# A new order for the first tile and for the end of attention, score blocks two in a row, and a second tile with plain fp32 projections

## The reference, cut to what matters

```python
x = x + tanh(g_xattn) * attention(layernorm(x), ctx, ctx, ctx)
x = x + tanh(g_ffn) * (layernorm(x).reshape(-1, 512) @ w.T)

def attention(q, k, c, s):
    qp = Wq @ instance_norm(q) + bq
    kp = Wk @ instance_norm(k) + bk
    sp = Ws @ s + bs
    attn = softmax(qp.T @ kp, axis=-1)          # 512 x 512 per batch
    mean = attn-weighted sum of sp
    mean_sq = attn-weighted sum of sp * sp
    std = sqrt(relu(mean_sq - mean * mean))
    return instance_norm(c) * std + mean

w = (weight_q - 8) * scales + zeros             # per group of 128 inputs
```

## Time and profile before

| quantity | value |
|---|---|
| median of three runs | 195.44 us |
| the profiled execution | 196.94 us |
| its span | 195.0 us |
| TensorE busy | 175.6 us (90%) |
| VectorE busy | 137.6 us (71%) |
| GpSimd busy | 132.9 us (68%) |
| ScalarE busy | 124.1 us (64%) |
| DMA, mean over the span | 50 GB/s |

### The profile page before, as it was taken

How to read it: one execution, slowest core, us unless ns; L and a number is a source line. 1 busy time by engine, 2 the same in 40 slices (tenths; PEclk the granted TensorE clock), 3 DMA queues, 4 the chain that set the end, 5 groups by cost and what they waited for, 6 DMA issues and landing times.

```text
span 195.0 us, 2721 instructions
## 1 busy us (share of the span) xinstructions
PE 175.6 (90%) x842; PEld 109.1 (56%) x842; DVE 137.6 (71%) x279; ACT 124.1 (64%) x268; POOL 132.9 (68%) x157
## 2 busy tenths in 40 slices
PE   6837996999999999999999999999997919898993
PEld 6525674564665656566565655654652418655681
DVE  2897577877878787787778779757624849777751
ACT  2327587777886977778697777869795194322420
POOL 1347369568868858896885888998998677445400
PEclk9997599999999999999999999999999997999999
DMA  5990031023004002200000000000000000111122
GB/s 174 365 363 6 0 124 42 2 56 105 0 3 163 0 0 55 110 0 2 3 0 0 2 0 3 0 0 0 2 0 3 0 0 0 54 54 54 57 108 108
DMA packets 4717, 9.83 MB, mean 50 GB/s; under 512 B 480, under 2 KB 608, under 8 KB 4704
## 3 DMA queue, kind: packets, MB, share of 16 engines
q1 hardware_dynamic: 4704, 9.67, 14.0%
HBM read 7.57 MB, written 2.10 MB: 50 GB/s over the span
## 4 chain that ended last, share of the span: by engine, by line
PE 64%; POOL 17%; DVE 14%; issue 3%; ACT 1%; POOLq 0%; DVEq 0%
PE pv_bank L281 20%; PE score L257 13%; PE turn_bank L267 13%; DVE X L648 4%; PE proj_bank L291 4%; POOL CTX L807 4%; POOL probs L730 3%; PE turn_bank L297 3%; DVE stats L653 3%; POOL rstd L811 2%; DVE neg_max L537 2%; PE proj_bank L242 2%; POOL w_lo L758 2%; PE score L348 2%; POOL w_deq L753 1%
## 5 line engine op out<-in xcount | busy, mean ns | idle before, releaser
L281 PE MATMUL pv_bank<-probs_t,values 128*128 128x512 f32 x120 | 58.8, 595 | 1.4 <-ACT VAR L398 1.4
L730 POOL TENSOR_SCALAR probs<-probs,rden 128x512 f32<-128x512 f32 x64 | 48.4, 762 | 8.8 <-DVE rden L542 8.7
L380 ACT ACTIVATE probs<-score,neg_max 128x512 f32<-128x512 f32 x64 | 44.7, 699 | 6.1 <-DVE neg_max L537 5.3
L389 ACT COPY probs_t<-turn_bank 128x512 f32<-128x512 f32 x64 | 37.3, 584 | 16.0 <-PE turn_bank L267 15.9
L537 DVE TENSOR_REDUCE neg_max<-score 128x2 f32<-128x1024 f32 x32 | 39.0, 1218 | 6.4 <-PE score L257 6.1
L267 PEld LDWEIGHTS turn_bank<-ident,probs 128*128 128x128 f32 x256 | 30.9, 145 | 15.0 <-issue 11.6
L267 PE MATMUL turn_bank<-ident,probs 128*128 128x128 f32 x256 | 37.8, 282 | 0.8 <-POOL probs L730 0.5
L281 PEld LDWEIGHTS pv_bank<-probs_t,values 128*128 128x128 f32 x120 | 19.4, 191 | 10.6 <-issue 10.3
L542 DVE RECIPROCAL rden<-den 128x1 f32<-128x1 f32 x64 | 9.8, 154 | 19.2 <-ACT probs L380 19.0
L257 PEld LDWEIGHTS score<-k_hi,q_hi 64*128 64x128 f32 x64 | 6.2, 186 | 25.8 <-ACT probs L380 14.9
L441 ACT ACTIVATE probs_t<-X,shift,rstd 128x512 f32<-128x512 f32 x8 | 6.5, 816 | 21.9 <-POOL shift L814 21.9
(11 more groups left out here) (83 smaller groups left out, 311.6 us busy)
## 6 DMA issues: line engine op xcount, KB each, us to landing
X<-in_x SPq DMA_DIRECT2D x8, 256.0 KB, 6.3
raw_ctx<-in_context SPq DMA_DIRECT2D x8, 256.0 KB, 3.1
sz<-in_scales_zeros SPq DMA_DIRECT2D x4, 512.0 KB, 4.4
out<-probs_t SPq DMA_DIRECT2D x8, 256.0 KB, 2.0
w_int<-in_weight_q_t SPq DMA_DIRECT2D x1, 1024.0 KB, 8.7
params_sb<-in_params SPq DMA_DIRECT2D x1, 226.0 KB, 3.9
```

Source lines behind the costliest of these rows:

```text
L281: mm = pe.matmul(sums_bank(t, b)[:, :], values[t % 2][:, i, b, :, :].rearrange("p a c -> p (a c)"), probs_t[t % 2][b][:, i, :], start=(i = ...
L380: act.activation(probs[c % PROBS][:, :], score[g % 2][:, N * b:N * b + N], ACT.Exp, bias=neg_max[:, g % 4, b:b + 1], accum_out=den[:, g % ...
L389: act.copy(probs_t[t % 2][b][:, :, P * j:P * j + P], turn_bank[b][:, :].rearrange("p (i n) -> p i n", i=JC)).then_inc(turned_kept, 1)
L730: pool.tensor_scalar(probs[c % PROBS][:, :], probs[c % PROBS][:, :], rden[:, g % 4, b:b + 1], 1.0, ALU.mult, ALU.mult).then_inc(probs_done, 1)
```

## The change

The edits fall into five groups.

- In TensorE's program the scores of two blocks are issued in a row at every even block, `scores(g + 2)` and `scores(g + 3)`, and none at the odd ones. ScalarE's order inside a block becomes exponential, copy, exponential, copy.
- The first tile is written out by hand on all engines. The fourteen identity products at the start are ten. `turn(0, 0)` to `turn(1, 1)` come before tile 1's first scores.
- Tile 1 too has plain fp32 projections (`PLAIN = 2`), so it has no `x_high`, `ctx_high`, `x_low` and `ctx_low`.
- The dequantisation of the weights is spread over tiles 2 to 7.
- At the end of attention the last tile's batch 0 is summed in `proj_bank` and batch 1 in `pv_bank` (before: the other way round), `turn_y(0)` stands before the last `weigh`, the orders on VectorE, ScalarE and GpSimd are new, and `y`, `result` and the feed-forward's banks have four buffers each where they had two.

The core of the diff:

```diff
-            for _ in range(14):
+            for _ in range(WARM):                      # WARM = 10
...
-            project_first()
+            pe.wait_ge(params_loaded, DMA)
+            project_q_plain(0)
+            project_k_plain(0)
             scores(0)
             scores(1)
+            project_q_plain(1)
+            scores(2)
+            turn(0, 0)
+            scores(3)
+            turn(0, 1)
+            project_k_plain(1)
+            turn(1, 0)
+            turn(1, 1)
...
-                    if g + 2 < PAIRS:
+                    if j % 2 == 0 and g + 2 < PAIRS:
                         scores(g + 2)
+                        scores(g + 3)
...
-            return proj_bank if (t, b) == (TILES - 1, 1) else pv_bank
+            return proj_bank if (t, b) == (TILES - 1, 0) else pv_bank
...
+            for i in range(JC):
+                weigh(TILES - 1, 0, i)
+            for i in range(JC - 1):
+                weigh(TILES - 1, 1, i)
             turn_y(0)
+            weigh(TILES - 1, 1, JC - 1)
             turn_y(1)
...
             for u in range(TILES):
+                add_ffn(u)
+                if u + 2 < TILES:
+                    keep_y_lo(u + 2)
+                if u == 0:
+                    with_mean(TILES - 1)
+                if u + 5 < TILES:
+                    after_attention(u + 5)
+                    row_statistics(u + 5)
+                    finish_statistics(u + 5)
```

More of the change, by code:

```diff
@@ L28, in gated_attention_ffn @@
     PROBS = 6
+    PLAIN = 2
+    WARM = 10
     assert 2 * C == P and N == 512 and JC == 4 and TILES == 8
@@ L105, in gated_attention_ffn @@
         proj_bank = banks("proj_bank")
-        ffn_bank = [score[i][:, 0:512] for i in range(2)]
+        ffn_bank = [score[i][:, n:n + 512] for n in (0, 512) for i in range(2)]
         params_loaded = sem("params_loaded")
@@ L112, in gated_attention_ffn @@
         sz_loaded = [sem(f"sz_loaded{g}") for g in range(GROUPS)]
-        stored = [sem(f"stored{i}") for i in range(2)]
+        stored = [sem(f"stored{i}") for i in range(4)]
         power_ready = sem("power_ready")
@@ L322, in _ @@
                         weigh(t - 1, j // 2, 1)
-            for b in range(2):
-                for i in range(JC):
-                    weigh(TILES - 1, b, i)
             def turn_y(u):
@@ L588, in _ @@
             keep_q_lo(0)
+            keep_k_lo(0)
+            normalise_x(1)
+            dve.wait_ge(w_hi_ready, 1)
+            dve.tensor_tensor(w_qk_lo[:, :, :], w_qk, w_qk_hi[:, :, :].bitcast(F32),
+                              ALU.subtract).then_inc(w_split, 1)
+            maximum(0)
+            maximum(1)
+            reciprocal(0, 0)
             ctx_statistics(1)
             ctx_variance(1)
-            keep_k_lo(0)
+            reciprocal(0, 1)
             ctx_shifted(1)
-            normalise_x(1)
-            x_high(1)
-            dve.wait_ge(gates_ready, 1)
-            maximum(0)
+            maximum(2)
+            reciprocal(1, 0)
+            reciprocal(1, 1)
             normalise_ctx(1)
-            ctx_high(1)
-            maximum(1)
-            reciprocal(0, 0)
-            reciprocal(0, 1)
-            reciprocal(1, 0)
+            keep_q_lo(1)
+            maximum(3)
+            reciprocal(2, 0)
+            x_statistics(2)
+            x_variance(2)
+            reciprocal(2, 1)
+            x_shifted(2)
+            keep_k_lo(1)
+            reciprocal(3, 0)
+            ctx_statistics(2)
+            ctx_variance(2)
             for t in range(TILES):
@@ L629, in _ @@
                             normalise_x(t + 2)
-                    if not later and j in (0, 2):
-                        scale_weights((t - TILES + 2) * 2 + j // 2)
                     if g + 2 < PAIRS:
                         reciprocal(g + 2, 0)
-                    if not later and j in (1, 3):
-                        weights_hi((t - TILES + 2) * 2 + j // 2)
                     if j == 2 and later:
@@ L640, in _ @@
                         ctx_high(t + 2)
+                    if j == 1 and t in (2, 4):
+                        scale_weights(t // 2 - 1)
+                    if j == 1 and t in (3, 5):
+                        weights_hi(t // 2 - 1)
+                    if j == 1 and t >= TILES - 2:
+                        scale_weights(t - TILES + 4)
+                    if j == 2 and t >= TILES - 2:
+                        weights_hi(t - TILES + 4)
                     if j == 0 and t >= 2:
@@ L793, in _ @@
                         square_values(t)
-                    if not later and j in (0, 2):
-                        dequantise((t - TILES + 2) * 2 + j // 2)
                     if g + 2 < PAIRS:
                         normalise_probs(g + 2, 0)
-                    if not later and j in (1, 3):
-                        weights_lo((t - TILES + 2) * 2 + j // 2)
                     if j == 2 and later:
@@ L803, in _ @@
                         ctx_low(t + 2)
+                    if j == 1 and t in (2, 4):
+                        dequantise(t // 2 - 1)
+                    if j == 1 and t in (3, 5):
+                        weights_lo(t // 2 - 1)
+                    if j == 1 and t == TILES - 2:
+                        dequantise(2)
+                    if j == 2 and t == TILES - 2:
+                        weights_lo(2)
+                    if j == 1 and t == TILES - 1:
+                        dequantise(3)
+                    if j == 2 and t == TILES - 1:
+                        weights_lo(3)
             def scale_context(u):
```

190 lines of the change are left out of this document (98 added, 92 removed).

## The result

The changed kernel takes 180.36 us, the median of four runs (179.7 to 181.18), against 195.35 (195.07 to 195.51) of the kernel before on the same chip. The ratio is 0.9226, with a 95% interval of 0.9178 to 0.9274. Predicted were 183.7 us and 181.0 to 187.7: faster as forecast, but by 3.3 us more, and outside the range.

What follows compares the result with a forecast made beforehand. TensorE was taken to bound the middle, with waste at both ends. Savings of 0.6 (start), 0 (middle), 6.5 (end of attention) and 4.6 us (feed-forward), 11.7 together, took the 195.44 us median to 183.7, range 181.0 to 187.7.

Steps and rivals of the forecast that it cites:

- The middle: TensorE-bound stage from tile 2's q projection to the scores of block 30: two score blocks in a row save 0 us.
- the slack I had called thin: In the middle, the second score block's buffer is free about 0.5 us early, about 0.4 in a tile's second half.
- The start: First tile up to tile 2's q projection: 1.7 us saved at full clock, 0.6 after 1.1 for half clock.
- the stretch: TensorE at half clock somewhere between 16 and 25 us in the first tile, costing 1 to 2 us, taken as 1.1.
- no half clock in the start: Rival: the first tile runs at full clock, giving 1.1 us back, 182.6 us in all; chance 0.17.
- the warm-up: Ten identity products end at 5.65 instead of 7.30 us; rival that first projections then run at 1.2 GHz: 186.0 us, chance 0.09.
- The end of attention: From the scores of block 30 to the first feed-forward product: 21.4 us instead of 27.97, saving 6.5.
- the wait for the bank: At the end of attention, TensorE's 1.36 us wait for ScalarE's copy before the last tile's `weigh` is gone.
- The feed-forward: Last stage: TensorE's pace of 3.26 us a round replaces a 4.13 us VectorE and GpSimd loop, saving 4.6 us.
- the crowding: In the feed-forward, VectorE instructions stretched beside GpSimd products cost 1.0 us, bounds 0 and 4.
- The rival with VectorE as the bound at 4.0 a round: VectorE, pushed by GpSimd, sets the feed-forward's pace for six rounds: 3.5 us more, 187.2 us; chance 0.15.

## Why the prediction was wrong

**The middle** is the step that failed. I took it at 0 on the sentence "No order can shorten that stage while its products stay the same", with one price for a score block and one for a projection wherever they stand. The conclusion followed only if prices do not depend on the neighbour, and the rows had the opposite in them: the q projection behind scores is 0.42 and two more parts up to 49.77, which is 0.23 each. I added the three to 0.89 and went on. The change takes 12 visits to the scores out of this stage (11 pairs where there were 23 single blocks), at 4.42 / 12 = 0.37 each; undoing the pairs made the middle 4.64 us longer, and the surcharge went when the scores used all rows. The rest of the step held: in the middle no second block waits for exponentials, and the slack I had called thin is thin, since the old order on ScalarE uses it up.

**The start** had its mechanism right and its sizes off, 1.27 us against 0.6. The q projection of tile 2 came at 31.30 (31.05 replayed at full clock, with 1.1 added 32.15). `scores(4)` was at 21.01 and not 21.65, 0.64 earlier; but eight profiles with this same first tile have it anywhere from 20.96 to 21.61, so this term is no larger than the spread between executions. From there on the replay has 9.4 us at full clock where the runs without the stretch show 8.72: 0.7, about two visits again. Against these the stretch cost 1.56 and not 1.1, and the extra block is worth 0.70 and not 0.89. 1.7 + 0.64 + 0.68 - 1.56 - 0.19 = 1.27. The stretch lay where forecast, between 16 and 25 us to within one, but my rival "no half clock in the start" at 0.17 was not a rival kernel: it is what happens in about half of the executions of this one. I also misread the warm-up: I put its products at 1.2 GHz because they take 0.207 us each, but the profile gives a granted clock of 1.00 there, as it does where the same products take 0.118 each as fillers (24 in 2.84 us). Why they are slower at the start is open.

**The end of attention** came at 21.69 us, 21.4 forecast, with `turn_y(1)` and the first product 0.3 us later than replayed. The account of why was partly wrong. I counted the wait for the bank as gain; put back it costs 1.9 us here and returns 1.4 in the feed-forward. The sum of both stages was right, the split was not a property of each edit. What else made up the 6.28 us, the spread dequantisation and the new orders on ScalarE, VectorE and GpSimd among it, was not taken back one by one and stays argued.

**The feed-forward** came at 27.46, 27.15 forecast: TensorE's pace of 3.24 a round (3.26), two waits of 0.86 together for the crowding that I took at 1.0 within 0 and 4. The rival with VectorE as the bound at 4.0 a round is out for all rounds but one (4.11, with the next at 3.74), and VectorE is the next limit: with 0.68 us more on it for each of two rows TensorE waits once more.

**The sum.** 11.7 us forecast, 15.0 between the medians and 16.07 between the profiled executions, of which 1.08 is the choice of executions. By stages the difference to 16.07 is 4.42 for the middle, 0.67 for the start, less 0.22, 0.27 and 0.23 for the two last stages and what lies outside. The range was open downward only to a full clock and no crowding, since for the middle I had bounds of 0 and +2 us. A bound below nothing was called for: a stage with TensorE busy throughout excludes a gain from waits, not one from cheaper products.

## What to carry to other kernels

An engine that is busy for a whole stage can still have its products made cheaper by their order: list each kind of product by what stands before it, and where the first behind a change of shape costs more, count the changes. Group the products that use part of the array, here two score blocks in a row for 0.37 us a visit saved. And before counting a removed wait as gain, ask which chain sets the end behind it: here 2.2 us of wait were worth some 0.5.

## What the runs showed of the hardware

- Each change between products over 64 rows, two side by side, and products over 128 costs TensorE 0.15 to 0.20 us: 0.18 on a pair's way in, 0.15 on a turn behind scores (0.59 against 0.44), 0.20 on a projection's first product (0.43 against 0.23) and on the value product (1.09 against 0.89). It counts as busy time, so no view of waits shows it.
- The same program has its half-clock stretch, 0.50 for some 3.4 us, in some executions and not in others, four of nine here. One profile may show either.
- VectorE's stretched instructions beside GpSimd are not only those with two SBUF inputs: the relu, which has one, took 1.50 us in place of 0.42.
